# Cross-attention with a mixture of experts behind it: POOL's splits set between its sums, loads in the order of their need, the last step's sums on TensorE and its split on VectorE, and the choices spread over more iterations

## The chip, the core and the metric

One core of one Trainium2 chip. The metric is the device time of one execution in microseconds; a profiled execution gives the trace. Engines: PE is TensorE (matmuls, transposes), DVE is VectorE, ACT is ScalarE, POOL is GpSimd, SP only issues DMAs.

## The reference, cut to what matters

Eight sequences of 224 tokens of 512 values go through one decoder layer: self-attention, cross-attention on 750 context rows with 16 heads and a linear distance bias, and a mixture of eight experts of which each token takes two.

```python
x = x + attn(layernorm(x))
q = (layernorm(x) @ Wq + bq); k, v = split(ctx @ Wkv + bkv)
scores = q @ k.T * scale - slope[h] * abs(key - query - (750 - 224))
x = x + softmax(scores) @ v @ Wo + bo          # cross-attention
s = layernorm(x) @ Wr.T + br                   # router, 8 experts
idx = top_k(s + biases_N, 2); w = softmax(s)[idx] / sum
x = x + sum_j w_j * ((silu(a) * b) @ Wl2[idx_j] + bl2[idx_j])   # a, b = h @ Wl1[idx_j] + bl1[idx_j]
```

## The kernel before, in words

Four stages run one after the other: opening (self-attention's projections), middle (self-attention, and the keys and values of the cross-attention), `cross_phase`, `moe_phase`. Only the last two are touched. All products of values that matter are made in three passes of a high and a low part ("split": ACT or POOL copies the high part, DVE or POOL subtracts it to get the low part).

`cross_phase` has 32 steps (`STEPS`): step s is batch s // 4 and head group s % 4, four heads hh each. In iteration s, TensorE (loop at L2003 to L2025) makes for each head the scores of step s + 1 laid out for ACT (`second_scores`, L1905 to L1911; ACT's `exp` is L2050) and those of step s + 2 laid out for their maxima (`first_scores`, L1884, L1888; DVE's `maxima` is L2155). After the four heads come `values(s)`: the value products (L1934), `turn_max(s + 2)` (L1920), which stands once in each step and marks its beginning in the trace, and the sums of the probabilities (L1944). Iteration s lies between the L1920 of s + 1 and that of s + 2. There are three score banks for each of the two layouts.

POOL's `sums` adds the probability tiles of a step (L1752, and L1756 up to `STORING` = 25; from then on TensorE adds two of them itself), so four heads times two additions. DVE's `normalise(s - 1)` (L2168, L2172) stands at the end of its iteration s and writes `o_f`. POOL's `split_o` (L1763, L1765) splits that. `project_out(b)` on TensorE (L1957 to L1959) uses the four splits of a batch in iterations with s % 4 = 1, at heads 0 and 2. DVE's `residual` (L2184) and `moments` (L2189, L2192) stand in the same iteration, `hidden` (L2200) in the one with s % 4 = 2, with TensorE's `turn_h` (L1981) and `route` (L1998) after it.

The choice of experts is made on DVE while the steps run: `choose(b0, b1, part)` in five parts (L2215 to L2232), `ranks` on TensorE (L1970 to L1972), `slots` (L2248 to L2266), `weights` (L2276 to L2286). For the first 12 tiles, `store_entries` on POOL writes 24 table entries by indirect DMAs (L1794). All of DVE's small operations there wait for one another.

SP issues the loads in program order: `load_qk(s)` has three pairs of q (L1638) and k (L1640) and waits for the scores of step s - 4, `load_v(s)` has two parts (L1650). Before the loop come `r_bias`, `c_bias`, `wr_raw` (L1687 to L1689), `load_qk(4)`, `load_v(3)`, `w_raw` (Wo, L1692) and `out_bias` (L1693). ACT splits `w_raw` in iteration 3 (L2097) and DVE in the same iteration (L2305).

After step 31 DVE adds the bias to the last x, splits quarters 0 and 1 of the first expert's weights (`split_w1`, L2291), normalises steps 30 and 31, chooses, and makes the last residual and hidden; then the table is read (L1714), rows of the first experts' step are fetched by POOL (L1800) and turned on TensorE (L2034). `moe_phase` begins with TensorE's ranks (L2647). In its opening DVE alternates between the first step's work (`add_bias` L2855, `multiply` L2861, `gated_lo` L2865), the table of the other tiles (`slots`, `weights`), and the low halves of the down weights (L2875).

## Time and profile before

| | us |
|---|---|
| median of 3 runs (lowest to highest) | 1781.89 (1773.87 to 1784.19) |
| profiled run | 1781.67 |
| its span, first to last instruction | 1780.0 |
| TensorE busy | 1685.4 (95%) |
| VectorE busy | 1075.7 (60%) |
| ScalarE busy | 748.0 (42%) |
| GpSimd busy | 751.6 (42%) |
| mean granted TensorE clock | 0.973 of full |
| cross-attention stage, from its first to its last step | about 680 to 1163 |

Times in the trace count from the span's start. Matmuls are pipelined, so the durations of neighbours overlap and what counts is from start to start. The idle time of an engine stands in brackets behind the instruction that ended it, with what released it. The granted clock is 1.00 for 2.4 GHz and 0.50 for 1.2 GHz.

### The profile page before, as it was taken

How to read it: one execution, taken by the hardware profiler on the slowest of the kernel's cores; microseconds unless marked ns; L12 is line 12 of the kernel's file. 1: busy time of each engine (PE TensorE's matmuls, PEld its weight loads, DVE VectorE, ACT ScalarE, POOL GpSimd, SP SyncE). 2: the span in 40 equal slices, each digit the busy share in tenths (PEclk: the TensorE clock that was granted, in tenths of full speed). 3: DMA queues.
4: the chain of work that ended last, by engine and by line, in shares of the span. 5: the costliest groups of instructions: out<-in, count | busy, mean ns of one | idle time of the engine just before them, and what ended most of it. 6: DMA issues, size and time to landing. Idle time of an engine off the chain costs nothing. (4 is left out here: it accounts for less than half of the span.)

```text
span 1780.0 us, 34824 instructions
## 1 busy us (share of the span) xinstructions
PE 1685.4 (95%) x11064; PEld 1356.9 (76%) x11064; DVE 1075.7 (60%) x1895; ACT 748.0 (42%) x1345; POOL 751.6 (42%) x852
## 2 busy tenths in 40 slices
PE   7998999999999997998998998789999999999998
PEld 6887787887887776776776776578888888888876
DVE  5453565555556654877878887663664646445653
ACT  3224343344344425665655564522442424224441
POOL 3100323323333325977788656541542414115451
PEclk9999999999999997999999998989999999999999
DMA  7836766666576758997877766245673737346773
GB/s 216 254 134 170 205 185 179 184 177 173 165 196 176 197 148 162 188 221 157 172 152 164 154 150 157 85 126 169 187 245 101 242 102 241 105 133 212 235 251 89
DMA packets 211841, 309.52 MB, mean 174 GB/s; under 512 B 21856, under 2 KB 151600, under 8 KB 207232
## 3 DMA queue, kind: packets, MB, share of 16 engines
q1 hardware_dynamic: 191584, 232.40, 49.3%
q0 software_dynamic: 15392, 41.02, 10.4%
q10 hardware_dynamic: 4752, 34.61, 5.3%
q8 instruction: 68, 1.11, 0.3%
q14 instruction: 45, 0.37, 0.1%
HBM read 224.30 MB, written 83.66 MB: 173 GB/s over the span
## 5 line engine op out<-in xcount | busy, mean ns | idle before, releaser
L2155 DVE TENSOR_REDUCE part_max<-a_s_bank 112x1 f32<-112x500 f32 (+1 forms) x368 | 225.3, 671 | 61.5 <-PE a_s_bank L1884 41.8
L2050 ACT ACTIVATE a_prob<-a_st_bank 125x448 f32<-125x448 f32 x384 | 196.7, 546 | 117.8 <-PE a_st_bank L1905 93.8
L2855 DVE TENSOR_TENSOR e_u_sb<-e_u_bank,e_b_row 128x512 f32<-128x512 f32 x134 | 92.4, 689 | 231.7 <-PE e_u_bank L2612 216.4
L2610 PE MATMUL e_u_bank<-e_w_hi,e_xT_hi 128*128 128x512 f32 x536 | 215.3, 402 | 0.9 <-DVE e_w_lo L2848 0.4
L2611 PE MATMUL e_u_bank<-e_w_lo,e_xT_hi 128*128 128x512 f32 x536 | 210.9, 393 | 0.0
L2612 PE MATMUL e_u_bank<-e_w_hi,e_xT_lo 128*128 128x512 f32 x536 | 210.4, 392 | 0.0
L2671 ACT ACTIVATE e_g_hi<-e_g_bank 128x256 fp32r<-128x256 f32 x133 | 51.3, 386 | 342.0 <-PE e_g_bank L2619 334.5
L2772 POOL DMA_INDIRECT out<-l_rows,e_y_row x33 | 53.0, 1605 | 290.7 <-DVE l_rows L2898 162.8
L1752 POOL TENSOR_TENSOR a_part_sum<-a_prob 125x448 f32<-125x448 f32 x128 | 148.2, 1162 | 54.5 <-ACT a_prob L2050 53.4
L992 POOL TENSOR_TENSOR m_prob_sum<-m_prob 112x224 f32<-112x224 f32 x128 | 85.4, 671 | 161.8 <-ACT m_prob L1240 152.1
L2748 POOL TENSOR_TENSOR e_w_lo<-e_w_raw,e_w_hi 128x1024 fp32r<-128x1024 f32 x28 | 102.6, 3674 | 49.0 <-ACT e_w_hi L2681 49.0
L1756 POOL TENSOR_TENSOR a_part_sum<-a_part_sum,a_prob 125x448 f32<-125x448 f32 x100 | 116.0, 1160 | 14.7 <-ACT a_prob L2050 0.4
L2610 PEld LDWEIGHTS e_u_bank<-e_w_hi,e_xT_hi 128*128 128x128 f32 x536 | 101.3, 189 | 25.8 <-DVE e_xT_lo L2843 3.6
L2612 PEld LDWEIGHTS e_u_bank<-e_w_hi,e_xT_lo 128*128 128x128 f32 x536 | 101.3, 189 | 23.2
L2611 PEld LDWEIGHTS e_u_bank<-e_w_lo,e_xT_hi 128*128 128x128 f32 x536 | 101.3, 189 | 20.3
L2629 PE MATMUL e_y_bank<-e_w_hi,e_g_hi 128*128 128x512 f32 x264 | 115.5, 437 | 0.0
L2630 PE MATMUL e_y_bank<-e_w_lo,e_g_hi 128*128 128x512 f32 x264 | 104.0, 394 | 0.0
L2631 PE MATMUL e_y_bank<-e_w_hi,e_g_lo 128*128 128x512 f32 x264 | 103.8, 393 | 0.0
L1313 DVE SCALAR_TENSOR_TENSOR m_kt_lo<-m_o_bank,m_b_col,m_kt_hi 128x500 fp32r<-128x500 f32 x48 | 35.4, 738 | 89.8 <-ACT m_kt_hi L1249 89.8
L2861 DVE TENSOR_TENSOR e_g_sb<-e_gate,e_u_sb 128x256 f32<-128x256 f32 x134 | 63.6, 475 | 42.8 <-ACT e_gate L2666 29.9
L1240 ACT ACTIVATE m_prob<-m_st_bank 112x448 f32<-112x448 f32 x128 | 68.2, 541 | 47.1 <-PE m_st_bank L1133 47.0
L1934 PE MATMUL a_or_bank<-a_prob,a_v_sb 125*32 125x224 f32 x1536 | 82.6, 365 | 0.0
(413 smaller groups left out, 4368.7 us busy)
## 6 DMA issues: line engine op xcount, KB each, us to landing
e_w_raw<-L_ffn_Wl SPq DMA_DIRECT2D x96, 512.0 KB, 11.0
e_b_row<-L_ffn_bl ACTq DMA_DIRECT2D x33, 1024.0 KB
k<-m_kt_hi SPq DMA_DIRECT2D x48, 250.0 KB, 4.1
k<-m_kt_lo SPq DMA_DIRECT2D x48, 250.0 KB, 5.0
m_c_in<-ctx POOLq DMA_DIRECT2D x12, 896.0 KB, 6.7
v<-m_cv SPq DMA_DIRECT2D x48, 224.0 KB
a_v_sb<-v SPq DMA_DIRECT2D x32, 336.0 KB
m_q_st<-q SPq DMA_DIRECT2D x93, 112.0 KB, 3.1
```

The lines of the kernel that those rows point to most:

```text
L1752: pool.tensor_tensor(part_sum[w][:, hh, :, :], prob[w][:, hh, 0:2, :], prob[w][:, hh, 2:4, :], ALU.add).then_inc(sum_done, 1)
L1756: pool.tensor_tensor(part_sum[w][:, hh, :, :], part_sum[w][:, hh, :, :], prob[w][:, hh, 4:6, :], ALU.add).then_inc(sum_done, 1)
L2050: act.activation(prob[s % 2][:, hh, 2 * u:2 * u + 2, :], st_bank[n % SB][0:CR, 0:2 * S].rearrange("p (e q) -> p e q", e=2), ACT.Exp).then_ ...
L2155: dve.tensor_reduce(out, scores, AX.X, ALU.max).then_inc(s_free, 1)
L2610: pe.matmul(out, xT_hi[:, slot, k, :], w_h, start=(k == 0), stop=False)
L2611: pe.matmul(out, xT_hi[:, slot, k, :], w_l, start=False, stop=False)
L2612: last = pe.matmul(out, xT_lo[:, slot, k, :], w_h, start=False, stop=(k == KT - 1))
L2629: pe.matmul(y_bank[slot][:, :], g_hi[:, q % 2, t, :], w2_hi[:, q, t, :], start=first, stop=False)
L2630: pe.matmul(y_bank[slot][:, :], g_hi[:, q % 2, t, :], w2_lo[:, q, t, :], start=False, stop=False)
L2631: last = pe.matmul(y_bank[slot][:, :], g_lo[:, q % 2, t, :], w2_hi[:, q, t, :], start=False, stop=end)
L2748: pool.tensor_tensor(w2_lo[:, q, :, :], w2_raw[:, q, :, :], as_f32(w2_hi[:, q, :, :]), ALU.subtract).then_inc(w2_ready, 1)
L2855: dve.tensor_tensor(u_sb[:, q % 2, :, :], u_bank[q % 2][:, :].rearrange("p (h n) -> p h n", h=2), b1_row[:, slot, :, HC * q:HC * q + HC], ...
```

## The change

It does eight things. POOL's `split_o(s - 1)` in iterations 4, 8, ... 28 stands between the sums of heads 0, 1 and those of heads 2, 3. The first loads are reordered: `wr_raw` alone stays in front, `load_qk(5)` and `load_v(4)` go ahead of Wo, `out_bias` goes to SP's iteration 3, `r_bias` and `c_bias` to 5, the zeros to 12. POOL adds `out_bias` for batch 0 in iteration 4. The last step's probabilities are summed by TensorE alone. Steps 30 and 31 are split by DVE. The 16 entries of the first go are stored as 6, 6, 4 in iterations 27, 28, 29 (before: 4 each in 25 to 28), the 8 of the second as 2 and 6 in 29 and 30. `choose`, `slots` and `weights` of DVE stand elsewhere. At the end, the table is read and the first rows are fetched and turned earlier, moments are made tile by tile, and `split_w1(3)` goes into `moe_phase`, ahead of `slots()`.

```diff
-    GOES = {20: (0, 8), 28: (8, FIRST_TILES)}
+    GOES = {22: (0, 8), 28: (8, FIRST_TILES)}
+    STORED = {27: (0, 6), 28: (6, 12), 29: (12, 16)}
...
-                sp.dma_start(r_bias[:, :], b_route.partition_broadcast(QR)).then_inc(small_loaded, DMA)
-                sp.dma_start(c_bias[:, :], choice_bias.partition_broadcast(QR)).then_inc(small_loaded, DMA)
-                sp.dma_start(wr_raw[:, :], w_route).then_inc(small_loaded, DMA)
-                load_qk(SLOTS)
-                load_v(SLOTS - 1)
+                sp.dma_start(wr_raw[:, :], w_route).then_inc(wr_loaded, DMA)
+                for s in (SLOTS, SLOTS + 1):
+                    load_qk(s)
+                    load_v(s - 1)
                 sp.dma_start(w_raw[:, :, :], w_out.rearrange("(k p) n -> p k n", p=P)).then_inc(w_loaded, DMA)
-                sp.dma_start(out_bias[:, :], b_out.partition_broadcast(P)).then_inc(bias_loaded, DMA)
...
+                    if s == 3:
+                        sp.dma_start(out_bias[:, :], b_out.partition_broadcast(P)).then_inc(bias_loaded, DMA)
+                    if s == 5:
+                        sp.dma_start(r_bias[:, :], b_route.partition_broadcast(QR)).then_inc(small_loaded, DMA)
+                        sp.dma_start(c_bias[:, :], choice_bias.partition_broadcast(QR)).then_inc(small_loaded, DMA)
+                    if s == 12:
                         sp.wait_ge(zeros_ready, 1)
...
+                    if s >= 4 and s % 4 == 0:
+
+                        sums(s + 1, range(0, 2))
                         split_o(s - 1)
+                        sums(s + 1, range(2, 4))
+                        if s in STORED:
+                            store_entries(0, *STORED[s])
+                    else:
+                        if s + 1 < STEPS - 1:
+                            sums(s + 1)
+                        if s in STORED:
+                            store_entries(0, *STORED[s])
+                        if s == STEPS - 3:
+                            store_entries(1, 0, 2)
+                        if s == STEPS - 2:
+                            store_entries(1, 2, 8)
+                        if 0 < s < STEPS - 1:
+                            split_o(s - 1)
...
-                    if s == 3:
+                    if s == 4:
                         pool.wait_ge(bias_loaded, DMA)
                         add_out_bias(0)
...
+                    else:
+                        tiles = [(prob, t) for t in range(NK)]
...
-                for t in range(2):
-                    project_out(B - 1, t, 0, GROUPS - 1)
-                for t in range(2):
-                    project_out(B - 1, t, GROUPS - 1, GROUPS)
-                turn_h(B - 1)
-                route(B - 1)
+                project_out(B - 1, 0, 0, GROUPS - 1)
+                project_out(B - 1, 1, 0, GROUPS - 2)
+                project_out(B - 1, 0, GROUPS - 1, GROUPS)
+                project_out(B - 1, 1, GROUPS - 2, GROUPS)
+                pe.wait_ge(of_ready, STEPS)
                 pe.wait_ge(row_loaded[0], DMA)
...
+                turn_h(B - 1)
+                route(B - 1)
...
+                        if (s, hh) in ((13, 0), (13, 2), (14, 1), (14, 3), (15, 1)):
+                            choose(0, 2, 2 * (s - 13) + hh // 2)
+                        if s == 21:
+                            choose(2, 4, hh)
+                        if (s, hh) == (22, 0):
+                            choose(2, 4, 4)
                         if (s, hh) == (22, 3):
-                            slots(20, 4)
+                            slots(22, 0)
+                        if (s, hh) == (23, 1):
+                            slots(22, 1)
+                        if (s, hh) == (23, 3):
+                            slots(22, 4)
                         if (s, hh) == (25, 0):
-                            weights(20, 2)
+                            slots(22, 2)
+                        if s == 25 and hh:
+                            weights(22, hh - 1)
+                        if (s, hh) == (26, 1):
+                            slots(22, 3)
+                        if (s, hh) == (26, 3):
+                            weights(22, 3)
...
                 split_w1(0)
-
-                dve.wait_ge(pv_done, STEPS - 1)
-                split_w1(1)
                 normalise(STEPS - 2)
-                normalise(STEPS - 1)
-                scores_done(B - 2)
+                split_o(STEPS - 2)
+                dve.wait_ge(table_loaded, DMA)
...
+                split_w1(1)
+                normalise(STEPS - 1)
+                split_o(STEPS - 1)
+                scores_done(B - 2)
...
                 multiply(0, 1)
+                split_w1(0, HCH - 1)
                 slots()
```

## Rows read from the trace of the kernel before

**Rows 1.** Windows: length, engines' busy time (instructions), granted clock, DMA share, GB/s

```profile
core 0: us, PE busy (x) PEld busy (x) DVE busy (x) ACT busy (x) POOL busy (x), PEclk, DMA share, GB/s
756.84:773.40 16.56, 16.16 (x145) 12.46 (x142) 10.91 (x22) 9.46 (x16) 12.12 (x13) 1.00 1.08 215
773.40:786.41 13.01, 11.65 (x124) 9.15 (x125) 12.37 (x19) 8.77 (x17) 10.60 (x10) 1.00 1.09 234
786.41:798.39 11.98, 11.88 (x136) 9.72 (x132) 9.11 (x17) 7.04 (x13) 8.41 (x10) 1.00 1.07 222
798.39:808.88 10.49, 10.39 (x121) 8.24 (x118) 9.15 (x16) 7.04 (x13) 9.84 (x11) 1.00 1.07 193
...
743.49:756.84 13.35, 12.10 (x121) 9.66 (x118) 10.64 (x16) 7.25 (x13) 12.17 (x12) 0.87 1.11 180
808.88:830.05 21.17, 17.91 (x145) 13.48 (x141) 11.08 (x22) 9.46 (x16) 14.80 (x15) 0.92 0.58 122
865.57:910.17 44.60, 41.33 (x401) 32.75 (x398) 38.11 (x77) 25.36 (x45) 34.22 (x33) 0.96 0.75 159
950.54:1068.51 117.97, 108.08 (x1051) 84.35 (x1048) 98.19 (x186) 65.37 (x117) 77.67 (x78) 0.94 0.71 152
1082.31:1099.98 17.67, 14.76 (x139) 10.50 (x140) 15.77 (x31) 6.97 (x13) 9.55 (x11) 0.81 0.79 237
1099.98:1122.45 22.47, 18.63 (x160) 14.10 (x156) 13.55 (x38) 10.32 (x18) 9.14 (x10) 0.92 0.23 61
```

**Rows 2.** Timeline of TensorE: start, us, line, out<-in, count [idle before <-releaser]

```profile
746.47 0.48 PE L1884 MATMUL a_s_bank<-third 100*112 100x500 f32 x1 [1.15 <-DMA third<-k]
815.00 0.48 PE L1957 MATMUL a_s_bank<-a_w_hi,a_o_split 128*112 128x512 f32 x1 [2.85 <-POOL a_o_split L1765]
1106.20 0.68 PE L1957 MATMUL a_s_bank<-a_w_hi,a_o_split 128*112 128x512 f32 x1 [2.36 <-issue]
1144.19 0.77 PE L1957 MATMUL a_s_bank<-a_w_hi,a_o_split 128*112 128x512 f32 x1 [3.20 <-POOL a_o_split L1765]
1155.25 1.76 PE L1981 MATMUL a_st_bank<-ident,l_rows 112*128 112x112 f32 x8 [3.89 <-DVE l_rows L2200]
1164.86 0.55 PE L2647 MATMUL e_y_bank<-r_mask,l_earlier 112*112 112x32 f32 x2 [2.67 <-PEq L1628]
1187.33 0.44 PE L2619 MATMUL e_g_bank<-ident,e_g_sb 128*128 128x128 f32 x2 [1.08 <-DVE e_g_sb L2861]
```

**Rows 3.** Timeline of VectorE, single places

```profile
809.35 0.39 DVE L2172 TENSOR_TENSOR a_o_f<-a_or_bank,a_rinv 128x224 f32<-128x224 f32 x1
882.25 0.76 DVE L2232 TENSOR_TENSOR r_before<-r_before,r_mask 112x8 f32<-112x8 f32 x4
970.88 2.93 DVE L2232 TENSOR_TENSOR r_before<-r_before,r_mask 112x8 f32<-112x8 f32 x4
1092.15 2.50 DVE L2247 SCALAR_TENSOR_TENSOR r_before<-a_pad,r_before 1x1 f32<-1x1 f32 x1
1133.94 4.49 DVE L2291 TENSOR_TENSOR e_w_lo<-e_w_raw,e_w_hi 128x2048 fp32r<-128x2048 f32 x2 [0.52 <-ACT e_w_hi L2121]
1150.79 1.29 DVE L2184 TENSOR_TENSOR a_x_new<-a_s_bank,l_rows 112x512 f32<-112x512 f32 x2 [2.63 <-PE a_s_bank L1959]
```

**Rows 4.** Timeline of POOL, two places

```profile
814.29 0.66 POOL L1765 TENSOR_TENSOR a_o_split<-a_o_f,a_o_split 128x224 fp32r<-128x224 f32 x1
...
1144.29 0.95 POOL L1794 DMA_INDIRECT place_table<-a_entry,a_place  x1 [0.16 <-issue]
```

**Rows 5.** DMA issues of 675 to 780 us: KB of one, median us to landing

```profile
a_v_sb<-v SPq DMA_DIRECT2D x10, 336.0 KB
...
second<-k SPq DMA_DIRECT2D x6, 375.0 KB, 13.4
l_rows<-L_xattn_Wo SPq DMA_DIRECT2D x1, 1024.0 KB, 16.6
...
second<-q SPq DMA_DIRECT2D x6, 112.0 KB, 12.0
```

**Rows 6.** Timeline of ScalarE: its first split of Wo, step 3

```profile
731.64 0.63 ACT L2097 ACTIVATE a_w_hi<-l_rows 128x512 fp32r<-128x512 f32 x1
```

More of the change, by code:

```diff
@@ L1583, in cross_phase @@
         w_loaded = c.sem("a_w_loaded")
+        wr_loaded = c.sem("a_wr_loaded")
         small_loaded = c.sem("a_small_loaded")
@@ L1743, in add_out_bias, with sums @@
                                        ALU.add).then_inc(xb_ready, 1)
-                def sums(s):
+                def sums(s, heads=range(4)):
                     w = s % 2
-                    if s >= 2:
+                    if s >= 2 and 0 in heads:
                         pool.wait_ge(pv_done, s - 1)
-                    for hh in range(4):
+                    for hh in heads:
                         pool.wait_ge(st_free, st_at["s", s, hh, 1] + 1)
@@ L2371, in _ @@
                 split_w1(0)
-                dve.wait_ge(pv_done, STEPS - 1)
-                split_w1(1)
                 normalise(STEPS - 2)
-                normalise(STEPS - 1)
-                scores_done(B - 2)
-                for part in range(5):
-                    choose(B - 2, B - 1, part)
-                for t in range(2):
-                    residual(B - 1, t)
-                moments(B - 1)
-                hidden(B - 1)
+                split_o(STEPS - 2)
                 dve.wait_ge(table_loaded, DMA)
@@ L2389, in _ @@
                     dve.tensor_copy(x_row[:, st:st + 1], table_sb[:, st, 0:1]).then_inc(x_row_ready, 1)
-                for q in range(2, HCH):
-                    split_w1(q)
+                split_w1(1)
+                normalise(STEPS - 1)
+                split_o(STEPS - 1)
+                scores_done(B - 2)
+                for part in range(5):
+                    choose(B - 2, B - 1, part)
+                for t in range(2):
+                    residual(B - 1, t)
+                    moments(B - 1, (t,))
+                hidden(B - 1)
+                dve.wait_ge(xhi_ready, 1)
+                dve.tensor_tensor(xT_lo[:, 0, :, :], or_bank[1][:, :].rearrange("p (k n) -> p k n", k=KT), as_f32(xT_hi[:, 0, :, :]), ALU.subtract).then_inc(t_free, 1)
+                split_w1(2)
                 scores_done(B - 1)
```

87 lines of the change are left out of this document (30 added, 57 removed).

## Prediction

> **What bounds the kernel now.** I read, in this order, the page's busy shares and its clock line, the idle times of TensorE by line, the cross-attention steps as windows, and then the timelines around each long window. TensorE is busy 95% of the span, so time is only to be had where it idles or where its clock is halved. In the cross-attention a step has a natural length that depends on its place in a batch of four: 16.56 us where s%4 is 1 (with the output projection), 13.01 for 2, 11.98 for 3 and 10.49 for 0 (the first four of [rows 1]). The reader is to see the VectorE column there: 12.37 of 13.01 us in the step with s%4 = 2, against 9.11 of 11.98 and 10.91 of 16.56 in its neighbours. So VectorE and not TensorE sets the step with s%4 = 2, and the steps beside it have room.
>
> The other rows of that group are the steps that are longer than their like: step 4 by 2.9 us (13.35 against 10.49), step 9 by 4.6 (21.17 against 16.56), steps 13 to 15 together by 3.1 (44.60 against 41.55), steps 19 to 26 by 13.9 (117.97 against 104.1), step 28 by some 6.4 and step 29 by some 5.1 (their like taken 0.8 longer for the two more tiles of sums). In most of them the granted clock is below 1: a stall of 1 to 3 us is followed by a stretch at the half clock (1.2 GHz instead of 2.4), so a stall costs more than its own length. Together these are some 36 us. The page's chain of work is of no use here, since it ends in the experts' loop.
>
> **Splits between sums.** At step 9 TensorE waits 2.85 us for L1765, POOL's second half of split_o(7) [rows 2]. VectorE wrote o_f(7) at 809.35 + 0.39 = 809.74; POOL ended the split at 814.29 + 0.66, because sums(9) stood ahead of it [rows 3, 4]. With the split after two of the four heads, POOL is free at about 809 and ends it at about 810.9, before TensorE asks for it (812.15 = 815.00 - 2.85). The stall goes, and with it the halved clock behind it: 4.6 us, from a trace that shows 21.17 against 16.56. What is late next: nothing until values(9), 15 us on; the two heads of sums that now stand behind the split end at about 815.5. The wait is new for POOL: behind it are those two sums and, at step 28, the table entries. In the other six projections no such stall shows except a 2.36 us one at step 29, which is put down to no engine [rows 2], and which ACT and VectorE share; I leave that one standing. **-4.6 us.**
>
> **Loads by need.** The stall of 1.15 us at step 4 is a wait for the keys of step 6 [rows 2], and the half clock after it makes 2.9 us. Ahead of those keys 256 KB of bias are taken out, about 1.4 us at the 180 GB/s of that step, so this stall goes: -2.9. But the 1024 KB of Wo now stand behind one more step's loads: three times 375 and 112 KB, and 375 KB of v in two parts, the larger 336 KB [rows 5], some 1.9 MB and at 190 GB/s about 10 us. Wo landed at 707.3 + 16.6 = 723.9; it would land at about 734. ACT's first split of it ran at 731.64 without a wait [rows 6]. So ACT, VectorE (which waits for that split) and then TensorE are held some 2.5 us at step 3, to which part of a half clock may come. The two cancel. Bounds: -2.5 if Wo comes in time after all, +2.5 if a full half-clock stretch is added. Adding out_bias on POOL one step later comes out just before the first residual asks for it; the zeros, stored at step 12 instead of 4, lie beside other work. **0 us.**
>
> **Choices spread.** Before, choose(0,2) filled steps 13 and 14. Its parts 0 and 1 go in front of the residuals of step 13, where VectorE waits for the projection anyway: nothing. Parts 2 and 3 go to step 14, the one without room, and cost their length, 0.6 to 2.1 us; part 4 goes to step 15. Its four additions took 0.76 us in one place and 2.93 in another [rows 3], with about 1 us of usable room there. I take 1.3 + 0.5 in place of 3.1: **-1.3 us** (from -3 to +2).
>
> Steps 19 to 26 hold 13.9 us. Afterwards steps 19, 20 and 24 have nothing added. Step 21 takes parts 0 to 3, mostly in front of residuals: 0.3. Step 22, without room, takes part 4 at its higher price, since POOL does full sums there, 2.9, the first of the slots 0.3, and a short half clock 1: 4.2. There VectorE also waits for turn_h and ranks on TensorE, but row_maxima(24), queued behind it, is needed only after the value products, so this is covered; without that cover it would cost 1.5. Step 23 takes 2.4 us, of which about 1 is over its room. Step 26 takes two small pieces at the lower price, 1.0, since POOL does half as many sums from step 25 on, and step 25 costs 0.2. In all 6.7 in place of 13.9: **-7.2 us**. All at low prices it is -12, all at high prices +3.
>
> **Steps 27 to 29.** Entries are stored six at a time from step 27 on in place of four from 25. Each costs POOL about 1.25 us, but POOL has no full sums there. In step 28 one VectorE operation on a single element took 2.50 us [rows 3] while POOL ran four sums in a row; TensorE stood behind it. After the change POOL stops between the second and third sum to wait for o_f(27), so this operation can get through. I take **-2 us**, between -6 (the stall and its half clock gone) and +2 (POOL two entries later than before and the split late).
>
> **The end of the stage.** TensorE waits 3.20 us at 1144.19 for split_o(30), which stood behind the entries on POOL, whose last one was issued at 1144.29 [rows 2, 4]. Now VectorE splits both last steps, POOL doesn't sum the last one (four sums gone, 0.75 us of TensorE products added), and the last six entries go before. By my reckoning POOL ends split_o(29) at about 1138 and VectorE split_o(30) at about 1140, before values(31) ends at 1141.7. The projection starts there, 2.5 us earlier and at full clock, with perhaps a wait of 1 us for split_o(31), and ends at 1147.7 to 1148.5 in place of 1151.35. The residuals started at 1150.79 [rows 3]; now they are behind a choose that ends at 1147.9. The wait for h, 3.89 us at 1155.25 [rows 2], stays, but all of it is some 3 us earlier, and the 0.7 us xT_lo of VectorE is no more the last thing of the stage. Against that, the two table steps now stand ahead of normalise(31): if the entries land late, it waits. **-3 us**, bounds -4.5 and 0. The next stage's first matmul, at 1164.86 [rows 2], would be at 1162 if only this changed.
>
> **The split moved into the experts' stage.** split_w1(3) is now in front of slots() on VectorE. One such split takes 4.49 / 2 = 2.25 us [rows 3]. It is in time for its own user, but VectorE is the late one there: TensorE waits 1.08 us for it at 1187.33 [rows 2]. So the whole 2.3 us come through: **+2.3 us**, from +0.5 (TensorE's slack before it absorbs some) to +4 (a half clock behind it). This is what the earlier end of the stage pays for.
>
> **The sum** against the profiled run's 1781.67 us (its span is 1780.0, and 1.7 lie around it; the median of the runs shown is 1781.89, the same): -4.6 + 0 - 1.3 - 7.2 - 2 - 3 + 2.3 = -15.8, so **1766 us**.
>
> **The rivals.** (1) The small operations stay stretched: parts in steps 14, 22 and 26 each wait for a sum of POOL, and the choices win nothing, while the rest does. 1766 + 8.5 + 1 for one more half clock = 1776. For it: 2.93 us for four operations of 0.19. Against it: 0.76 for the same four elsewhere [rows 3].
> (2) Everything at its low price: -4.6 - 2.5 - 3 - 12 - 4 - 4 + 1 is -29, of which half-clock stretches that merely move give some back: 1756.
> (3) The change doesn't do what it says: POOL, waiting between the sums for o_f, or late with its entries, makes the split no earlier than TensorE's need, so steps 9 and the end gain nothing. 1766 + 4.6 + 3 = 1774. Against it: o_f(7) stood ready 4 us before POOL took it [rows 3, 4].
> (4) Slower than before: each of the some 22 small operations in steps 14, 15, 22, 23 and 26 waits for a whole sum of 1.15 us. That is about 25 us, with five half-clock stretches of 1.7 us 33 us, in place of 17 now; with the other parts' -7 the time would be 1791. It decides from about 0.74 us an operation on. The worst row has 2.93 / 4 = 0.73.
> A sentence of the Trainium skill speaks for (1) and (4) and against this placing: in SBUF - State Buffer, section SBUF: two separate sides, VectorE operations with two SBUF inputs and GpSimd operations that read SBUF share a port pair that is locked for a whole instruction, so the loser waits it out in full. By that rule, with POOL summing back to back in steps 14, 22 and 23, the time is the 1791 of (4); the 2.93 us row agrees with such a lock, the 0.76 us row shows that it isn't met every time.
>
> **How the numbers follow.** Forecast 0.48 (own range 1759 to 1773), (1) 0.18, (2) 0.14, (3) 0.12, (4) 0.08. The range 1756 to 1778 takes in (1), (3) and the near half of (2). This kernel can be told from no change at about 0.5%, or 9 us: faster than 1773 has the forecast, (2) and a little of (3), 0.66; within 0.5% 0.27; slower 0.07.
>
> **What would show it.** Right: no wait of TensorE for a split at step 9, and its length near 16.6; steps 19 and 20 near 12 and 10.5; a new wait of ACT for the Wo load in step 3; TensorE's wait before the last projection gone; the first wait of TensorE for e_g_sb in the experts' stage longer by 2 us. Wrong: steps 14, 22 and 26 longer than 16 us, a wait of ACT in step 3 beyond 4 us, POOL's split still last before a projection, or half-clock stretches that are as many as before in other places.

## The result

The changed kernel takes 1790.42 us in the median (1780.38 to 1801.57) against 1778.34 us (1772.85 to 1790.95) of the kernel before, timed together: a ratio of 1.0066, 95% interval 1.0047 to 1.0085. It is slower by 12 us; I had forecast 16 us faster. Its profiled execution took 1797.34 us, 7 above its own median, so a difference of the two traces overstates the change by some 4 us. First lines of its page (span; busy time and share by engine):

```profile
span 1795.7 us, 34858 instructions
PE 1689.9 (94%) x11080; PEld 1360.0 (76%) x11080; DVE 1078.0 (60%) x1899; ACT 747.6 (42%) x1345; POOL 740.6 (41%) x844
```

TensorE works 4.5 us more and the span is 15.7 longer: the rest is idle time. The windows of the same steps as in [rows 1], with step 3 ahead of them (columns as there):

```profile
727.75:745.44 17.69, 13.32 (x121) 10.51 (x118) 11.10 (x20) 8.82 (x17) 12.29 (x13) 0.81 1.09 178
745.44:755.93 10.49, 10.39 (x121) 8.23 (x117) 9.82 (x16) 7.03 (x13) 6.66 (x7) 1.00 1.10 178
755.93:775.57 19.64, 16.57 (x145) 12.55 (x141) 11.08 (x22) 9.49 (x16) 17.57 (x16) 1.00 1.08 202
811.05:827.67 16.62, 16.21 (x144) 12.44 (x140) 11.07 (x22) 9.45 (x16) 14.59 (x14) 1.00 0.63 134
863.19:912.62 49.43, 43.59 (x401) 33.17 (x398) 39.76 (x78) 25.56 (x45) 38.40 (x38) 0.93 0.72 152
952.74:1071.37 118.63, 106.54 (x1050) 84.94 (x1047) 99.94 (x187) 64.97 (x117) 75.45 (x75) 0.94 0.73 155
1084.80:1106.92 22.12, 19.98 (x139) 14.30 (x139) 14.11 (x31) 7.21 (x13) 8.07 (x10) 0.69 0.52 161
1106.92:1126.61 19.69, 17.21 (x161) 13.05 (x157) 14.85 (x38) 10.32 (x18) 15.39 (x17) 1.00 0.35 100
```

In order: steps 3, 4, 5, 9, 13 to 15, 19 to 26, 28, 29. Steps 4 and 9 are what I had said (10.49 and 16.62 in place of 13.35 and 21.17). Step 29 is 2.8 us shorter. Steps 3 and 5 are 4.5 and 3.1 us longer (step 3 took 13.18 us before), 13 to 15 together 4.8 longer where I had 1.3 shorter, 19 to 26 0.7 longer where I had 7.2 shorter. Step 28 is 4.5 longer at a mean clock of 0.69.

The stalls in TensorE's, VectorE's and ScalarE's timelines that answer to [rows 2, 3, 6]:

```profile
734.05 0.63 ACT L2113 ACTIVATE a_w_hi<-l_rows 128x512 fp32r<-128x512 f32 x1 [5.00 <-DMA l_rows<-L_xattn_Wo]
765.13 0.69 DVE L2200 TENSOR_TENSOR a_x_new<-a_s_bank,a_xh 112x512 f32<-112x512 f32 x1 [5.21 <-POOL a_xh L1747]
...
814.15 0.39 PE L1970 MATMUL a_s_bank<-a_w_hi,a_o_split 128*112 128x512 f32 x1
...
1159.74 0.48 PE L1970 MATMUL a_s_bank<-a_w_hi,a_o_split 128*112 128x512 f32 x1
1169.71 0.98 PE L1994 MATMUL a_st_bank<-ident,l_rows 112*128 112x112 f32 x8 [3.72 <-DVE l_rows L2216]
1177.79 0.55 PE L2667 MATMUL e_y_bank<-r_mask,l_earlier 112*112 112x32 f32 x2 [3.25 <-PEq L1630]
1197.01 0.44 PE L2639 MATMUL e_g_bank<-ident,e_g_sb 128*128 128x128 f32 x2 [1.89 <-DVE e_g_sb L2881]
```

Both waits for a split, 2.85 us at step 9 and 3.20 before the last projection, are gone. Yet the last projection starts 15.6 us later than before. Between step 29 and there lies something new. TensorE, VectorE, ScalarE and POOL around 1130 us, start and length first, idle time in brackets:

```profile
1133.09 0.35 PE L1958 MATMUL a_or_bank<-a_part_sum,a_ones 125*32 125x224 f32 x1 [0.18 <-issue]
1134.88 0.41 PE L1920 MATMUL a_st_bank<-a_rel_k,a_d_lo 125*125 125x224 f32 x1
1141.79 0.55 PE L1914 MATMUL a_st_bank<-a_q_st,a_k_st 104*125 104x224 f32 x1 [6.50 <-ACT a_prob L2066]
...
1139.72 1.56 DVE L2184 RECIPROCAL a_rinv<-a_or_bank 128x224 f32<-128x224 f32 x1 [10.15 <-remote]
...
1141.19 0.98 ACT L2066 ACTIVATE a_prob<-a_st_bank 125x448 f32<-125x448 f32 x2 [7.89 <-remote]
...
1132.46 0.95 POOL L1799 DMA_INDIRECT place_table<-a_entry,a_place  x1 [0.15 <-issue]
1133.72 0.96 POOL L1799 DMA_INDIRECT place_table<-a_entry,a_place  x1 [0.30 <-issue]
...
1138.72 0.94 POOL L1799 DMA_INDIRECT place_table<-a_entry,a_place  x1 [0.30 <-issue]
```

By their rows, the sums that VectorE's reciprocal reads were done at 1133.09 + 0.35 = 1133.4, and the scores for ScalarE's exponentials at 1135.3 (the first exponential reads only the first of three banks, which was done earlier). Neither engine starts. "remote" means that the profile ties the wait to no engine here. POOL issues six table entries in a row until 1139.66; VectorE starts at 1139.72 and ScalarE at 1141.19, 6.3 and 5.9 us later than these rows allow. At step 28 ScalarE waits 5.07 us until 1087.56, inside a run of six, and 3.68 us until 1092.15, 1.7 us after that run. TensorE's instructions come one by one there with gaps that nothing explains ("issue"), and VectorE waits for them:

```profile
1083.19 1.03 POOL L1799 DMA_INDIRECT place_table<-a_entry,a_place  x1 [0.18 <-issue]
...
1089.55 0.94 POOL L1799 DMA_INDIRECT place_table<-a_entry,a_place  x1 [0.30 <-issue]
...
1087.56 0.91 ACT L2058 ACTIVATE second<-a_st_bank 8x896 fp32r<-8x896 f32 x1 [5.07 <-remote]
...
1090.39 0.38 PE L1914 MATMUL a_st_bank<-second 104*125 104x224 f32 x2 [0.73 <-issue]
...
1092.12 1.85 DVE L2171 TENSOR_REDUCE part_max<-a_s_bank 112x1 f32<-112x500 f32 x3 [5.49 <-PE a_s_bank L1893]
```

The times at which the semaphores rose, which the same trace has, name the engine that is late. A semaphore is the counter by which one engine tells another that its work is done. `pv_done`, which TensorE raises at the end of a step's sums and for which the reciprocal and the exponential both wait, rises 0.40 us after the start of the last sum in 29 of the 31 places of this trace where TensorE ends such sums. In step 28 it rises 3.79 us after, and in step 30 6.61 us after, at 1139.70; VectorE starts 0.02 us later. The semaphores of the three banks of scores rise at 1141.11 to 1141.21, and ScalarE starts at 1141.19. ScalarE's waits that end at 1087.56 (5.07 us) and 1132.40 (6.32 us) end 0.02 us behind a semaphore of TensorE too. So ScalarE and VectorE don't stand still by themselves: they wait for TensorE, which reports work late that its rows show as started in time.

My leading theory, formed from the rows without these times, was: a run of entries on POOL holds the other engines until its end, and the change made the runs longer. The rival: the loads of the experts' weights, or where the instruction fetches fall, do it.

### The profile page after: what moved, and what is told of

Its sections match the earlier page's. It is cut to its first block and busy times, and to the rows that moved or that the text cites. A ratio compares the mean times of both kernels' runs of the same rounds, so it can differ in the third digit from the quotient of the medians.

```text
span 1795.7 us, 34858 instructions
## 1 busy us (share of the span) xinstructions
PE 1689.9 (94%) x11080; PEld 1360.0 (76%) x11080; DVE 1078.0 (60%) x1899; ACT 747.6 (42%) x1345; POOL 740.6 (41%) x844
## 5 line engine op out<-in xcount | busy, mean ns | idle before, releaser
L2171 DVE TENSOR_REDUCE part_max<-a_s_bank 112x1 f32<-112x500 f32 (+1 forms) x368 | 225.2, 670 | 62.7 <-PE a_s_bank L1893 46.6
L1757 POOL TENSOR_TENSOR a_part_sum<-a_prob 125x448 f32<-125x448 f32 x124 | 142.8, 1154 | 42.4 <-ACT a_prob L2066 42.0
L1761 POOL TENSOR_TENSOR a_part_sum<-a_part_sum,a_prob 125x448 f32<-125x448 f32 x100 | 116.5, 1165 | 14.6 <-ACT a_prob L2066 0.4
```

Of the source, the lines that this page charges most:

```text
L1757: pool.tensor_tensor(part_sum[w][:, hh, :, :], prob[w][:, hh, 0:2, :], prob[w][:, hh, 2:4, :], ALU.add).then_inc(sum_done, 1)
L1761: pool.tensor_tensor(part_sum[w][:, hh, :, :], part_sum[w][:, hh, :, :], prob[w][:, hh, 4:6, :], ALU.add).then_inc(sum_done, 1)
L2171: dve.tensor_reduce(out, scores, AX.X, ALU.max).then_inc(s_free, 1)
```

## Experiments

The lengths below are differences between starts of steps in each kernel's trace (one execution each); the ratio is to the kernel before, timed on the same chip. "End" goes from the start of step 30 to the first product of the experts' stage, "experts" from there to the end of the span.

| kernel | ratio (95% interval) | steps 3 to 5 | 9 | 13 to 15 | 19 to 26 | 28 | 29 | end | experts |
|---|---|---|---|---|---|---|---|---|---|
| before | 1 | 43.1 | 21.2 | 44.6 | 118.0 | 17.7 | 22.5 | 42.4 | 615.1 |
| after | 1.0066 (1.0047 to 1.0085) | 47.8 | 16.6 | 49.4 | 118.6 | 22.1 | 19.7 | 51.2 | 617.9 |
| b1_splits | 0.9952 (0.9934 to 0.9970) | 42.8 | 17.2 | 44.9 | 116.7 | 14.5 | 18.8 | 41.4 | 615.5 |
| b2_entries | 1.0051 (1.0033 to 1.0069) | 47.6 | 16.9 | 46.1 | 120.1 | 18.4 | 20.4 | 46.6 | 615.4 |
| b3_loads | 1.0000 (0.9986 to 1.0014) | 45.0 | 23.8 | 44.6 | 118.2 | 17.7 | 18.4 | 41.3 | 614.9 |
| a1_thin | 1.0015 (0.9999 to 1.0031) | 52.5 | 16.7 | 50.1 | 118.6 | 15.0 | 18.4 | 37.9 | 617.6 |
| c1_thin_oldchoices | 0.9995 (0.9977 to 1.0013) | 49.8 | 16.7 | 44.9 | 118.2 | 14.9 | 19.0 | 40.2 | 617.7 |
| c2_thin_bias | 0.9994 (0.9978 to 1.0011) | 47.7 | 18.2 | 49.1 | 116.0 | 16.6 | 18.4 | 39.8 | 617.1 |
| c3_end | 0.9973 (0.9953 to 0.9994) | 46.3 | 17.3 | 44.6 | 118.5 | 17.7 | 20.1 | 39.9 | 614.6 |
| c4_noentries | 0.9987 (0.9971 to 1.0004) | 50.5 | 16.6 | 50.2 | 115.8 | 14.6 | 18.4 | 37.1 | 616.4 |
| e1_part4 | 0.9973 (0.9951 to 0.9995) | 45.3 | 17.2 | 45.0 | 117.3 | 13.4 | 19.5 | 37.9 | 617.4 |
| e2_w1back | 0.9969 (0.9954 to 0.9984) | 43.5 | 18.0 | 49.5 | 118.7 | 15.0 | 18.4 | 37.9 | 614.9 |
| e3_splits_end | 0.9927 (0.9903 to 0.9952) | 43.0 | 17.6 | 44.9 | 116.7 | 15.0 | 18.4 | 37.9 | 614.4 |
| e4_best | 0.9922 (0.9894 to 0.9950) | 42.7 | 16.7 | 46.9 | 117.1 | 15.0 | 18.7 | 37.8 | 615.4 |
| f1_e3_thin | 0.9929 (0.9907 to 0.9952) | 43.3 | 20.9 | 44.7 | 117.3 | 13.4 | 19.5 | 37.4 | 615.0 |
| f2_best | 0.9942 (0.9919 to 0.9965) | 41.9 | 16.7 | 42.9 | 118.0 | 15.1 | 18.4 | 38.0 | 614.7 |

**b1_splits.** The kernel before with

```diff
-                    if s + 1 < STEPS:
-                        sums(s + 1)
+                    if s >= 4 and s % 4 == 0:
+                        sums(s + 1, range(0, 2))
+                        split_o(s - 1)
+                        sums(s + 1, range(2, 4))
```

> The kernel before with one part of the change alone: in the steps whose number is a multiple of four, POOL splits o_f after two of the four heads of sums. Theory A, the prediction's term: step 9 goes from 21.17 us to about 16.6 and nothing else moves, so the time is 4.6 us below the kernel before, a ratio of 0.9974. Rival B: the two heads that now stand behind the split, or the entries of the table behind those, come late at steps 4, 12 to 28, and some of the gain is lost; then step 9 is short as well but the ratio is 0.999 to 1.001.

Measured: 0.9952, 8.5 us, nearly twice the term. Step 9 gives 4.0 us, and steps 28 and 29 are 6.9 us shorter than in the kernel before (3.2 and 3.7). The part in step 29 may be one execution's luck, since b3_loads has 18.4 there without any edit. The part in step 28 isn't: VectorE's operation on one element that took 2.50 us [rows 3] takes 3.01 us in b3_loads and 2.71 in c3_end, which also keep the old place of the split and take 17.7 us for step 28. In b1_splits no such operation takes even 1 us, and the step takes 14.5.

**b2_entries.** The kernel before with

```diff
-                    if STORING <= s < STORING + 4:
-                        store_entries(0, 4 * (s - STORING), 4 * (s - STORING) + 4)
-                    if s == STEPS - 2:
-                        store_entries(1, 2, 7)
-                store_entries(1, 7, 8)
+                    if s in STORED:                    # {27: (0, 6), 28: (6, 12), 29: (12, 16)}
+                        store_entries(0, *STORED[s])
+                    if s == STEPS - 3:
+                        store_entries(1, 0, 2)
+                    if s == STEPS - 2:
+                        store_entries(1, 2, 8)
```

> The kernel before with only the grouping of the table's entries changed to that of the changed kernel: 6 from step 27, 6 from 28, 4 and 2 from 29, 6 from 30, in place of 4 in each of steps 25 to 28, 2 in 29, 5 and 1 in 30. Theory A, from the trace of the changed kernel, in which ACT and VectorE stand still for 5.1, 3.7, 6.3, 7.9 and 10.2 us and start again when POOL has issued the last entry of a run (1090.5, 1131.2, 1139.7): the run of entries itself holds the others, longer runs hold them longer, and the time is 5 to 10 us above the kernel before, a ratio of 1.003 to 1.0055. Rival B: the pauses come from the loads of the experts' weights (some 410 GB/s at 1130 us) or from where the instruction fetches happen to fall, and not from the entries; then the ratio is within 0.001 of 1.

Measured: 1.0051, 9 us slower, by the grouping and the place of the entries alone (in iterations 27 to 30 all of them now stand ahead of POOL's split). Its one trace is 4.3 us longer than that of before, and the end is where it shows: 46.6 us against 41.3 to 42.4. TensorE's last projection and POOL's entry before it:

```profile
1148.10 0.77 PE L1956 MATMUL a_s_bank<-a_w_hi,a_o_split 128*112 128x512 f32 x1 [8.15 <-POOL a_o_split L1766]
...
1144.32 0.94 POOL L1795 DMA_INDIRECT place_table<-a_entry,a_place  x1 [0.30 <-issue]
1145.27 0.38 POOL L1764 CAST a_o_split<-a_o_f 128x224 fp32r<-128x224 f32 x1
```

So in this kernel the entries cost plainly by their place: a split that TensorE waits for stands behind six of them, and the wait of 3.20 us [rows 2] becomes 8.15. That route doesn't exist in the changed kernel, where VectorE splits the last steps; the pauses must be told apart there. This trace doesn't have them, though it has six entries in each of four iterations: `pv_done` rises 0.40 us after the last sum in all 31 places. So the ratio is the one that theory A forecast, but by another route.

**a1_thin.** The changed kernel with the same 24 entries in the same iterations, one or two behind each head of sums:

```diff
+                def sums_and_entries(s, heads):
+                    at = 6 * (s - 27)
+                    for hh in heads:
+                        if s + 1 < STEPS - 1:
+                            sums(s + 1, (hh,))
+                        ...
+                        if 27 <= s <= 30:
+                            for n in ((0,), (1, 2), (3,), (4, 5))[hh]:
+                                ...
```

> The changed kernel with the same 24 entries in the same steps 27 to 30, but one or two at a time between the heads of sums instead of six in a row. Theory A (a run of entries holds ACT, VectorE and TensorE until its end): the pauses of steps 28 and 30 shrink to those of one or two entries (under 3 us), step 28 goes from 22.1 us to about 18 and the projection of the last batch starts some 7 us earlier; the time is 7 to 11 us below the changed kernel, which puts it at a ratio of 1.0005 to 1.003 to the kernel before (the changed kernel has 1.0066). Rival B (loads or instruction fetches make the pauses): the ratio stays at 1.005 to 1.008.

Measured: 1.0015, which is 9 us less than the changed kernel; the intervals don't touch. Steps 28, 29 and the end in its trace take 71.3 us in place of 93.0. That is 21.7 us where the medians give 9: its steps 3 to 5 are 4.7 us longer, and the trace of the changed kernel was one of its slower executions. `pv_done` is on time in all 31 places. In iteration 30, where no sums stand between, its six entries run with gaps of only 0.3 to 0.5 us (1129.78 to 1139.12), and no pause comes of it. Windows of steps 28 and 29, to compare with the last two of after above:

```profile
1092.06:1107.03 14.97, 13.74 (x139) 10.22 (x139) 13.28 (x29) 7.13 (x13) 7.61 (x9) 0.89 0.73 222
1107.03:1125.45 18.42, 16.94 (x160) 12.98 (x157) 15.18 (x40) 10.33 (x18) 14.58 (x15) 1.00 0.42 122
```

**c4_noentries.** The changed kernel with the calls of `store_entries` taken out, which leaves out the storing of the table.

> The changed kernel without the 24 indirect transfers that store the table's entries (that part of the computation is left out: the experts' first rows are then fetched from the table's zeros). Theory A (a run of these transfers on POOL holds ACT, VectorE and TensorE): no idle time above 2 us of ACT or VectorE in steps 28 to 30 but for their inputs, steps 28, 29 take about 14.5 and 18.4 us in place of 22.1 and 19.7, and the last projection starts 10 us earlier; the time is 10 to 16 us below the changed kernel (1.0066), a ratio of 0.9975 to 1.001. Rival B (loads or instruction fetches are the cause and the entries only bystanders): the pauses stay, and the ratio is 1.004 or more.

Measured: 0.9987, 14 us below the changed kernel. Steps 28 and 29, the same two windows:

```profile
1084.46:1099.09 14.63, 13.70 (x139) 10.30 (x139) 12.81 (x28) 7.18 (x13) 3.33 (x4) 0.88 0.70 222
1099.09:1117.52 18.43, 16.94 (x161) 12.99 (x158) 15.36 (x41) 10.33 (x18) 7.81 (x8) 1.00 0.42 124
```

They are those of a1_thin within 0.4 us, with the experts' loads in place (222 GB/s), and `pv_done` is on time in all 31 places. The entries are the cause of the pauses and the loads aren't. As for the fetches of instructions, no packet of the instruction queues falls between 1132.4 and 1142.4 us in the trace of the changed kernel, so the pause around 1139 doesn't end with one. Spread thin they cost some 5 us in all (1.0015 against 0.9987, intervals that overlap), in runs of six 14.

**b3_loads.** The kernel before with the new order of the first loads and `add_out_bias(0)` in iteration 4.

> The kernel before with only the loads by need: the keys of step 6 and 7 before Wo, the small biases and the zeros later, out_bias loaded in iteration 3 and added to xh one step later on POOL. From the trace of the changed kernel: step 4 -2.9 us, step 3 +4.5 (ACT waits 5.0 us for Wo), step 5 +3.1 (VectorE's first residual waits 5.2 us for the sum of xh and out_bias). Theory A: these three are this part's, so the time is 3 to 5.5 us above the kernel before, a ratio of 1.0017 to 1.003. Rival B: step 5 is late only because POOL splits between the sums there (sums of step 5 stand behind the split); without that the addition comes in time and the ratio is 1.000 to 1.001.

Measured: 1.0000. Rival B holds: step 5 takes 16.8 us here. (Step 9 takes 23.8 us, since POOL's split stands behind all four heads of sums and TensorE waits 4.51 us for it.) And steps 3 to 5, 45.0 us, lie between b1_splits (42.8) and b2_entries (47.6) or c3_end (46.3), three kernels that have the old order of loads. In b2_entries TensorE waits in step 3, and at step 5 for the split (timeline of TensorE):

```profile
732.47 0.76 PE L1883 MATMUL a_s_bank<-second 100*112 100x500 f32 x1 [2.45 <-DMA second<-k]
...
760.90 0.49 PE L1956 MATMUL a_s_bank<-a_w_hi,a_o_split 128*112 128x512 f32 x1 [1.92 <-POOL a_o_split L1766]
```

The late load isn't tied to step 4, where my one trace had it; in other executions of the same orders it stops step 3, step 4 is then short, and TensorE reaches the projection of step 5 before POOL's split.

**c2_thin_bias.** a1_thin with

```diff
                         split_o(s - 1)
+                        if s == 4:
+                            pool.wait_ge(bias_loaded, DMA)
+                            add_out_bias(0)
+                            load_x(1)
                         sums_and_entries(s, range(2, 4))
```

> The changed kernel with thin entries, and the sum of xh and out_bias for batch 0 on POOL moved from behind the second pair of sums of step 5 to in front of it, right behind the split. Theory A: the 5.2 us wait of VectorE for it at step 5, which holds TensorE 2.7 us, goes and step 5 takes 16.6 us in place of 19.6 to 22.2; the time is 3 to 5 us below a1_thin (1.0015), a ratio of 0.999 to 1.0. Rival B: the two heads of sums behind it are now as late as it was, and the ratio stays at 1.001 to 1.002.

Measured: 0.9994, 3.7 us below a1_thin, and step 5 takes 16.75 us in place of 22.20. The difference of the two ratios is within its error; the step's length is what speaks for theory A. VectorE's first residual now waits for TensorE alone:

```profile
768.90 0.69 DVE L2203 TENSOR_TENSOR a_x_new<-a_s_bank,a_xh 112x512 f32<-112x512 f32 x1 [2.31 <-PE a_s_bank L1975]
```

**c1_thin_oldchoices.** a1_thin with `choose`, `slots`, `weights` and `score_exp` where the kernel before has them.

> The changed kernel with thin entries (the run a1_thin, ratio 1.0015), and the choices, slots and weights put back where the kernel before has them (iterations 13, 19 to 22, 24, 25; scores' exponentials at 23). Theory A (the small VectorE operations cost more where the change put them): in the traces steps 13 to 15 are 4.8 us longer and steps 19 to 26 0.7 us longer than before, so this kernel is some 5.5 us below a1_thin, a ratio of 0.9985 (0.9975 to 0.9995). Rival B: the two placings are worth the same and the 5.5 us are an accident of one execution; then the ratio is 1.001 to 1.002. By my prediction's terms (-1.3 and -7.2 for the new placing) it would be 8.5 us slower than a1_thin, 1.0063.

Measured: 0.9995, 3.6 us below a1_thin where my terms put it 8.5 above. The 3.6 us can't be told from nothing (the error is 4), but the forecast 8.5 the other way is excluded. Steps 13 to 15 take 44.9 us in place of 50.1. Steps 19 to 26 are the same within 0.5 us: the new placing moved their loss, it didn't lower it.

**e1_part4.** c2_thin_bias with

```diff
-                        if (s, hh) in ((13, 0), (13, 2), (14, 1), (14, 3), (15, 1)):
+                        if (s, hh) in ((13, 0), (13, 2), (14, 1), (14, 3)):
...
+                        if (s, hh) == (15, 0):
+                            choose(0, 2, 4)
                         if s + 2 < STEPS:
                             maxima(s + 2, hh)
```

> The kernel of c2_thin_bias (ratio 0.9994) with one thing moved: the four dependent additions of the last part of the first choice stand at the start of iteration 15, in front of the maxima, where POOL has no sums to do, and not behind the second maxima, where POOL runs sums back to back. Theory A (each small VectorE operation waits for POOL's running instruction to end: 0.45 us for the first two and 2.13 us for the last two, beside three sums of 1.13 us): they take some 0.8 us there and lie in VectorE's idle 1.6 us; step 15 goes from 16.2 us to 12.0, and the time is 4 us below c2, a ratio of 0.9965 to 0.998. Rival B (the four additions cost TensorE their place in the queue wherever they stand in this step): step 15 stays above 14 us and the ratio at 0.999 or more.

Measured: 0.9973, 3.7 us below c2, within the error of the two ratios; step 15 takes 11.99 us in place of 16.16, which is what speaks for theory A. VectorE's four additions and POOL beside them, in the changed kernel (first three lines) and here:

```profile
903.43 2.62 DVE L2257 TENSOR_TENSOR r_before<-r_before,r_mask 112x8 f32<-112x8 f32 x4
903.79 1.14 POOL L1761 TENSOR_TENSOR a_part_sum<-a_part_sum,a_prob 125x448 f32<-125x448 f32 x1
904.89 1.13 POOL L1757 TENSOR_TENSOR a_part_sum<-a_prob 125x448 f32<-125x448 f32 x1
```

```profile
890.99 1.29 DVE L2260 TENSOR_TENSOR r_before<-r_before,r_mask 112x8 f32<-112x8 f32 x4
891.14 0.37 POOL L1768 CAST a_o_split<-a_o_f 128x224 fp32r<-128x224 f32 x1 [0.92 <-DVE a_o_f L2191]
891.59 0.67 POOL L1770 TENSOR_TENSOR a_o_split<-a_o_f,a_o_split 128x224 fp32r<-128x224 f32 x1
```

Beside the sums they end at 903.43 + 2.62 = 906.05, when the second of the two sums shown ends (906.02). After that TensorE waits 2.30 us for the maxima queued behind them (at 906.92). Beside the shorter split they take half as long, and they lie in idle time. The Trainium skill, SBUF - State Buffer, section SBUF: two separate sides, has just this as an exclusive lock of a port pair for a whole instruction; the two traces agree.

**e2_w1back.** c2_thin_bias with `split_w1(3)` back at the end of the cross-attention.

> The kernel of c2_thin_bias (ratio 0.9994) with the split of the experts' weights, chunk 3, put back into the end of the cross-attention's stage. Theory A: from the first product of the experts' stage to the end takes 617.1 to 617.9 us with it there and 614.6 to 615.5 without, so the time is 2.5 us less, and nothing waits for VectorE at the end of the cross-attention; a ratio of 0.998. Rival B: the next stage starts later by the 2.2 us of the split, and the ratio is unchanged at 0.9994.

Measured: 0.9969, 4.4 us below c2. In the traces the experts' stage is 2.2 us shorter and the end is no longer (37.9 against 39.8). TensorE's wait for e_g_sb is 0.70 us in place of 1.86, so 1.2 of the 2.2 us; where the other 1.0 goes wasn't followed up.

**c3_end.** The kernel before with the last step's sums by TensorE, the last two splits and the table's rows on VectorE ahead of `split_w1(1)`, and the new order at the end; `split_w1(3)` stays.

> The kernel before with only the end of the stage changed: the last step's sums by TensorE, both last splits and the table's rows before split_w1(1) on VectorE, the last projection in the new order, all 8 late entries by iteration 30 (5 and 1 become 6 in a row); the split of the experts' weights stays in this stage. Theory A, the prediction's term: 3 us below the kernel before (0 to 4.5), a ratio of 0.9983. Rival B: the six entries in a row hold ACT and VectorE, and what the split gains is lost; the ratio is 0.9995 to 1.002. Right if no wait for o_split stands before the last projection.

Measured: 0.9973, 4.8 us. No wait stands before the last projection:

```profile
1140.84 0.48 PE L1958 MATMUL a_s_bank<-a_w_hi,a_o_split 128*112 128x512 f32 x1
1150.82 1.75 PE L1982 MATMUL a_st_bank<-ident,l_rows 112*128 112x112 f32 x8 [3.72 <-DVE l_rows L2204]
```

Its trace also has a run of six entries back to back in iteration 30, where the changed kernel has the longest pause. ScalarE makes its twelve exponentials beside it without a stop (first and last entry of the run):

```profile
1123.10 5.65 ACT L2054 ACTIVATE a_prob<-a_st_bank 125x448 f32<-125x448 f32 x12 [2.08 <-PE a_st_bank L1908]
...
1123.73 0.94 POOL L1794 DMA_INDIRECT place_table<-a_entry,a_place  x1 [0.16 <-issue]
...
1130.98 0.94 POOL L1794 DMA_INDIRECT place_table<-a_entry,a_place  x1 [0.30 <-issue]
```

So a run of six doesn't hold the others by its length alone. Something else, which no run isolates, must come with it.

**e3_splits_end.** b1_splits and c3_end together.

> The kernel before with two parts of the change together: the splits between the sums (alone 0.9952) and the end of the stage (alone 0.9973), the rest as before. Theory A: the two touch different steps and add up, a ratio of 0.9925. Rival B: six entries in a row at iteration 30 or four at 28 hold the splits again and part is lost, 0.995.

Measured: 0.9927, 13 us below the kernel before, the sum of the two (8.5 + 4.8). It beats both kernels.

**e4_best, f1_e3_thin, f2_best.** e3 with thin entries and the first choice's parts 2 to 4 at the start of iteration 15; with thin entries alone; with thin entries and part 4 alone there.

> The kernel of e3_splits_end with the table's entries one behind each head of sums in iterations 25 to 28 and spread in 30, and the first choice's parts 2 to 4 at the start of iteration 15, in front of the maxima, in place of iteration 13. Theory A: thin entries are worth 1 to 4 us here, where runs have four and not six, and steps 13 to 15 go from 44.9 us to about 42, so the time is 4 to 7 us below e3, a ratio of 0.989 to 0.991. Rival B: with four entries in a row there was little left to win, and the thin ones stop POOL's sums; the ratio is that of e3 or above.

> The kernel of e3_splits_end (0.9927) with the table's entries spread, one behind each head of sums in iterations 25 to 28, two at 29, one or two at a time at 30, and nothing else. Theory A (a run of entries holds the other engines in proportion to its length, and only where they need something new in it): runs of four held ACT 1.6 to 1.8 us each in e3 and cost TensorE nothing, so there is little to win, a ratio of 0.991 to 0.993. Rival B: spreading entries is worth as much here as it was in the changed kernel (9 us), 0.988. If it is above 0.994, the thin entries hold POOL's own sums.

> The kernel of f1 with only the last part of the first choice moved from iteration 13 to the start of iteration 15, in front of the maxima; parts 2 and 3 stay in 13. In e4 three parts stood at the start of iteration 15 and made step 15 16.24 us long (12.0 without), which took back what steps 13 and 14 won; in e1 the last part alone stood there and step 15 took 11.99. Theory A (the idle 1.6 us of VectorE there holds one part and not three): step 13 goes from 18.2 us to about 17.4, step 14 from 14.7 to about 13, step 15 stays at 12.0; 2.5 us below f1, a ratio of 0.990 to 0.9915. Rival B: steps 13 and 14 stay as they are, the maxima behind the residuals being what holds them, and the ratio is that of f1.

Measured: 0.9922, 0.9929, 0.9942; none can be told from e3. With runs of four there was nothing more for thin entries to win (f1, theory A's ratio; in the traces of e3 and f1 alike, `pv_done` is on time in all 31 places). In e4 the three parts won 2.3 us in steps 13 and 14 and lost 4.2 in step 15. In f2 steps 13 to 15 took 42.9 us in place of 44.7, as theory A said, but the time doesn't show these 2 us. Nor do the splits between the sums always do what they should. At step 9 of f1, TensorE waits 2.46 us for the split, because POOL had stood still before:

```profile
793.36 0.68 POOL L1740 DMA_DIRECT2D a_xh<-x  x1 [7.47 <-issue]
...
810.61 0.49 PE L1970 MATMUL a_s_bank<-a_w_hi,a_o_split 128*112 128x512 f32 x1 [2.46 <-POOL a_o_split L1767]
```

## Why the prediction was wrong

Term by term, what I forecast and what the runs gave, in us:

| term | forecast | measured | from |
|---|---|---|---|
| splits between sums | -4.6 | -8.5 | b1 |
| loads by need | 0 | 0 alone; +3.7 with the splits | b3; a1 less c2 |
| choices | -8.5 | +3.6 | a1 less c1 |
| steps 27 to 29, entries | -2 | +9 | b2; after less a1 |
| end of the stage | -3 | -4.8 | c3 |
| split of the weights moved | +2.3 | +2.2 to +4.4 | c2 less e2 |
| sum | -15.8 | +5 to +7 | |
| the whole | -15.8 | +12 | |

Most ratios to the kernel before carry an error of 3 to 4 us and each difference of two ratios one of 4 to 5, and the terms were taken on different kernels, so the 5 us that the sum is short of +12 aren't assigned to anything.

Two steps of the prediction failed in their mechanism, the entries and the choices, and they make up 23 of the 28 us between forecast and result (11 and 12).

**Steps 27 to 29, the entries: the mechanism failed.** I wrote that each entry "costs POOL about 1.25 us, but POOL has no full sums there", so I costed it on POOL alone and at nothing for the others. The trace of before had the sign of it: ScalarE idle in step 29, and [rows 2] the 2.36 us that were "put down to no engine" and that "ACT and VectorE share". I left that one standing instead of asking what POOL did then. It issued the last of four entries, and ScalarE and VectorE went on beside it (trace of before):

```profile
1104.74 0.94 POOL L1794 DMA_INDIRECT place_table<-a_entry,a_place  x1 [0.30 <-issue]
1105.33 0.98 ACT L2050 ACTIVATE a_prob<-a_st_bank 125x448 f32<-125x448 f32 x2 [4.05 <-remote]
1105.37 1.26 DVE L2155 TENSOR_REDUCE part_max<-a_s_bank 112x1 f32<-112x500 f32 x2 [4.33 <-DMA first<-k]
```

Here too the semaphores of TensorE rise late: `pv_done` 2.19 us after the start of the last sum in place of 0.40, those of the scores at 1105.24 to 1105.36, though the first of these products started at 1101.91. What the term left at nothing is this cost to the other engines: in the changed kernel 9 us by the spreading of the entries (a1_thin) and 14 us by their absence (c4_noentries). It should have been a rival. The other half of the term, that VectorE's one-element operation of step 28 gets through, was right, and belongs to the split between the sums, which alone brings it (3.2 us of b1_splits).

**Choices: the mechanism was that of my rivals (1) and (4), the size near (1).** Steps 13 to 15 and 19 to 26 together were 17 us over their natural length before and are 22.4 after; I had forecast 8.5 less, rival (1) none less, rival (4) 33. So the measured 1790 us lies beside the 1791 of rival (4) by luck: the choices lost a third of what (4) adds, and most of the rest is the entries, which no rival had. I gave each small operation a price between 0.19 and 0.73 us and took something near the low end where I saw "room". The row with 2.93 us for four [rows 3] was the nearer one for the place that I followed, step 15, where POOL runs sums back to back: 2.62 us. Room counted as a step's idle time isn't room either. In step 15 VectorE has 2.9 us without work, but most of it lies before the maxima and the operations stood behind them, so TensorE waited 2.30 us and then ran at half clock: 4.3 us for operations of 0.8. I had written 0.5. For steps 14, 22 and 26 the mark that I set, 16 us, was passed by all three (16.42, 18.78, 16.82). The gain of 13.9 to 6.7 us in steps 19 to 26 came out as 13.9 to 14.5.

**Loads: right alone, wrong in company.** Wo landed at 734.05, as worked out. ScalarE's wait for it was 5.0 us and not 2.5, beyond the 4 us that I had set as a sign of being wrong, since TensorE and so ScalarE came there earlier. The sentence "Adding out_bias on POOL one step later comes out just before the first residual asks for it" failed: I had moved that addition past split_o, but not past the two heads of sums that the same change puts behind the split, 4.8 us (four operations of 1.15 and their gaps). With them ahead of it, VectorE waits 5.21 us for it; with the addition in front of them, VectorE waits for TensorE alone (c2).

**Splits between sums: right, too small.** The 4.6 us came (4.0 in b1, 4.5 in the changed kernel), but I took step 9 as the only place. Some 3 us more came in step 28, as said, and up to 3.7 in step 29, of which luck is a part. Step 5 is another place where the split can be late: in the trace of before it had no wait for the split, where a wait for keys in step 4 had given POOL time, and two executions of the same order of loads without that stall show 1.92 us (b2, c3). Rival (3) fell.

**The end of the stage: right, a little too small.** In c3_end there is no wait before the projection, the wait for h is still 3.7 us, and VectorE doesn't wait at the table steps. Its gain was hidden in the changed kernel by the pauses just ahead of it.

**The split of the weights: right in size.** The experts' stage is 2.2 us longer with it in the traces (c2 against e2); the 4.4 us of the ratios lie just beyond my bound of 4, within their error. The sign that I had named was missed: TensorE's first wait for e_g_sb was to be 2 us longer and went from 1.08 to 1.89.

## What to carry to other kernels

Cost a moved instruction against everything that the same change puts in front of it on its queue, and not against the old queue. Read an idle time that no engine is named for by asking which engine was busy just until its end, and when the semaphore that was waited for rose: the first points at a cause, the second names the engine that is late. Where two engines are in each other's way, a small operation can cost several times its own length (0.66 us an addition in place of 0.19), so place it where the other engine is idle; and before trusting a stall in a stretch that runs at the speed of its loads, see whether a second execution has it in the same step.

## What the hardware showed

Beside indirect transfers on POOL, TensorE can be late in reporting its work. In the changed kernel a semaphore of TensorE rose 6.61 us after the start of the last product that raises it, in place of 0.40, while POOL issued six transfers in a row. VectorE went on 0.02 us after it. Without the transfers, or with them spread, those pauses are gone and the kernel is 14 and 9 us faster (in c1, with them spread, the longest that is left is 1.62 us for 0.40). The transfers are needed for the pauses but don't suffice: the runs of six in b2 and c3 and that with short gaps in a1 delayed no such semaphore, while a run of four delayed one by 1.8 us (2.19 for 0.40) in the kernel before. What else must come with them is open and wasn't tried, and so is whether the products or only their reports are late. It doesn't look like the lock above, since the late engine is TensorE, and by the same section of the Trainium skill ScalarE and TensorE never wait at those ports.

Second, a stall at the loads wanders: eight kernels that have the old order of loads took 41.9 to 47.6 us for steps 3 to 5.
